# A two-layer graph network kernel: statistics a step ahead, transposes in the middle of aggregates, copies ahead of relus, adjacency chunks 4 to 6 issued behind DMA transposes

## The reference, cut to what matters

```python
def layer0(h, adj, s, weight, wgt_alpha, act_alpha, act_alpha2):
    w_norm   = (weight - mean(weight)) / std(weight, ddof=1)
    weight_q = weight_quant(w_norm, wgt_alpha, 3 bits)     # integers -7..7 times a step
    xq       = act_quant(h, act_alpha, 4 bits)             # integers up to 15 times a step
    support  = relu(xq @ weight_q)                         # 2048 x 512
    sup_q    = act_quant(support, act_alpha2, 4 bits)
    return adj @ sup_q                                     # 2048 x 2048 x 512

h = maximum(layernorm(x), 0);  x = x + layer0(h, adj, ...)
h = maximum(layernorm(x), 0);  x = x + layer1(h, adj, ...)
```

## Time and profile before

| | |
|---|---|
| runs, us | 157.33, 157.59, 158.1 |
| the profiled execution | 158.1 us, span 156.3 us, mean granted clock 0.986 |
| PE, PEld | 141.1 us (90%), 110.9 us (71%) |
| DVE, ACT, POOL | 108.5 us (69%), 108.3 us (69%), 30.1 us (19%) |
| moved by DMA | 27.44 MB, mean 176 GB/s |

### The profile page before, as it was taken

One profiled execution on the slowest core, in us unless ns is written; L12 is line 12 of the kernel. 1 busy time (PEld: TensorE's weight loads), 2 busy tenths in 40 slices (PEclk: granted clock), 3 DMA queues, 4 the chain that ended last, 5 costly groups with the idle time before them and its releaser, 6 DMA issues.

```text
span 156.3 us, 2088 instructions
## 1 busy us (share of the span) xinstructions
PE 141.1 (90%) x704; PEld 110.9 (71%) x704; DVE 108.5 (69%) x210; ACT 108.3 (69%) x137; POOL 30.1 (19%) x57
## 2 busy tenths in 40 slices
PE   0399999898999999999999999999999999999930
PEld 0395756565757667888888888888888888889920
DVE  0789978995966439997853686696779778624451
ACT  3587896896998779805955999999997977011000
POOL 2351232332020000016100101101105256011010
PEclk9999999999999999999999999999999999999995
DMA  5999999993315100080199899997101101110102
GB/s 146 331 420 423 396 388 419 430 306 38 67 38 67 34 0 0 0 273 0 17 268 415 258 361 376 377 351 268 69 0 67 71 0 67 67 67 0 67 8 71
DMA packets 11837, 27.44 MB, mean 176 GB/s; under 512 B 5040, under 2 KB 5296, under 8 KB 9776
## 3 DMA queue, kind: packets, MB, share of 16 engines
q1 hardware_dynamic: 11680, 27.01, 51.2%
q10 hardware_dynamic: 144, 0.26, 0.7%
HBM read 22.03 MB, written 4.19 MB: 168 GB/s over the span
## 4 chain that ended last, share of the span: by engine, by line
PE 72%; DVE 9%; DMA 7%; issue 6%; ACT 2%; POOL 1%; POOLq 0%; ACTq 0%; DVEq 0%
PE acc L930 26%; PE acc L932 26%; PE acc L912 7%; PE acc L913 6%; PE acc L898 5%; DMA h_iT<-h_i 4%; DMA w_sb<-weight 2%; DVE st L686 2%; DVE lo L721 1%; PE acc L940 1%; DVE w_st L749 1%; ACT hi L351 1%; ACT ring L371 1%; DVE h_i L710 1%; DVE mv L691 1%
## 5 line engine op out<-in xcount | busy, mean ns | idle before, releaser
L930 PE MATMUL acc<-sup,hi 128*128 128x512 f32 (+1 forms) x208 | 76.4, 374 | 0.1
L932 PE MATMUL acc<-sup,lo 128*128 128x512 f32 (+1 forms) x208 | 76.2, 373 | 0.0
L930 PEld LDWEIGHTS acc<-sup,hi 128*128 128x128 f32 x208 | 39.2, 188 | 7.3 <-issue 0.5
L932 PEld LDWEIGHTS acc<-sup,lo 128*128 128x128 f32 x208 | 39.2, 188 | 6.8
L363 ACT ACTIVATE junk<-raw,below 128x2048 uint8<-128x2048 f32 x16 | 31.8, 1985 | 0.0
L726 DVE TENSOR_TENSOR lo<-raw,hi 128x2048 fp32r<-128x2048 f32 x11 | 25.2, 2288 | 7.0 <-ACT hi L356 7.0
L912 PE MATMUL acc<-sup,hi 128*128 128x512 f32 x64 | 27.4, 428 | 0.7 <-DVE sup L715 0.7
L398 ACT ACTIVATE ring<-x_sb,nm 128x512 f32<-128x512 f32 x15 | 10.5, 716 | 23.1 <-POOL nm L509 19.6
L509 POOL TENSOR_SCALAR nm<-mv 128x1 f32<-128x1 f32 (+1 forms) x12 | 10.2, 847 | 83.4 <-DVE ve L696 83.4
L913 PE MATMUL acc<-sup,lo 128*128 128x512 f32 x64 | 25.1, 392 | 0.0
L356 ACT ACTIVATE hi<-raw 128x2048 fp32r<-128x2048 f32 x11 | 20.9, 1904 | 0.2 <-PE acc L913 0.2
(11 more groups left out here) (66 smaller groups left out, 83.1 us busy)
## 6 DMA issues: line engine op xcount, KB each, us to landing
raw<-adj_t SPq DMA_DIRECT2D x16, 1024.0 KB, 7.1
out<-ring SPq DMA_DIRECT2D x15, 256.0 KB, 4.9
x_sb<-x SPq DMA_DIRECT2D x3, 1024.0 KB, 14.0
w_sb<-weight SPq DMA_DIRECT2D x4, 258.0 KB, 4.3
x_sb<-x SPq DMA_DIRECT2D x1, 512.0 KB, 6.2
x_sb<-x ACTq DMA_DIRECT2D x1, 256.0 KB, 4.0
x_sb<-x SPq DMA_DIRECT2D x1, 256.0 KB, 5.3
out<-ring SPq DMA_DIRECT2D x2, 128.0 KB, 2.4
```

Of the source, the lines that this page charges most:

```text
L930: nc.tensor.matmul(bank[:, cols], part(hi, k % PARTS, j), sup[:, j, cols], start=(j == 0), stop=False)
L932: ins = nc.tensor.matmul(bank[:, cols], part(lo, k % PARTS, j), sup[:, j, cols], start=False, stop=(j == T - 1))
```

## The change

- VectorE: stats(7) and normalise(5) come ahead of the loop, right behind stats(6), and quantise_sup(2) ahead of quantise_h(4); in steps 4 and 5 the statistics are one tile further on, step 4 does quantise_sup(3) before two of them, step 5 one ahead of quantise_sup(4). From step 6 on the order is as before.
- ScalarE: split_piece(3) goes ahead of relu1(4); in steps 4 to 7 split_piece(j) goes between relu_sup(j-1) and copy_T(j), ahead of the relu1s of the step.
- PE: in steps 4 to 7 the transposes of tile j stand in the middle of aggregate_first(j-2), between rows 0, 1 and rows 2, 3. aggregate_first and aggregate do all hi matmuls of their rows (or of the tile) first and wait for the lo part only then.
- SP: only chunk 3 is issued ahead of the DMA transposes; chunks 4, 5 and 6 are issued behind transposes 8, 9 and 10.

```diff
             load_x(5)
-            for k in range(3, RAW):
-                load_adj(k)
+            load_adj(3)
             for j in range(TURN, T):
                 sp.wait_ge(hq_ready, j + 1)
                 if j >= TURN + 2:
                     sp.wait_ge(hqT_ready, j - 1)
                 sp.dma_start_transpose(h_iT[:, j % 2, :, :], h_i[:, j % SLOTS, :]).then_inc(h_turned[j % 2], 16)
+                if j - TURN + GT < RAW:
+                    load_adj(j - TURN + GT)
...
             copy_T(2)
             copy_T(3)
+            split_piece(3)
             relu1(4)
             relu_sup(2)
             relu1(5)
-            split_piece(3)
             for j in range(4, T + 2):
                 if j <= T:
                     relu_sup(j - 1)
+                if j < TURN:
+                    split_piece(j)
                 if j < T:
                     copy_T(j)
...
-                if j < T - 2:
+                if TURN <= j < T - 2:
                     split_piece(j)
-                elif j <= T:
+                elif T - 2 <= j <= T:
...
             lo_of_piece(2)
             stats(6)
+            normalise(5, stats(7))
+            quantise_sup(2)
             quantise_h(4)
-            quantise_sup(2)
-            nxt = 7
+            nxt = 8
...
-                for n in range(2 if j <= 5 else 1):
-                    if n == 1:
-                        quantise_sup(j - 1)
+                if j == 4:
+                    quantise_sup(j - 1)
+                for _ in range(2 if j == 4 else 1):
                     if nxt < T:
...
-                if 5 < j <= T:
+                if 4 < j <= T:
                     quantise_sup(j - 1)
...
                 pe.wait_ge(hi_piece, j + 1)
+                for t in rows:
+                    at = (j % GT) * GT + t
+                    nc.tensor.matmul(acc[t][:, :], part(hi, k % PARTS, at), sup[:, j, :], start=(j == 0), stop=False)
                 pe.wait_ge(lo_piece, j + 1)
                 for t in rows:
                     at = (j % GT) * GT + t
-                    nc.tensor.matmul(acc[t][:, :], part(hi, k % PARTS, at), sup[:, j, :], start=(j == 0), stop=False)
                     ins = nc.tensor.matmul(acc[t][:, :], part(lo, k % PARTS, at), sup[:, j, :], start=False, stop=(j == T - 1))
...
-                if j % GT == GT - 1 and j < T - 1:
+                if j % GT == GT - 1 and j < T - 1 and rows[-1] == GT - 1:
                     ins.then_inc(chunk_used, 1)
...
                 wait_hi(pe, k)
-                wait_lo(pe, k)
...
                         nc.tensor.matmul(bank[:, cols], part(hi, k % PARTS, j), sup[:, j, cols],
                                          start=(j == 0), stop=False)
+                    wait_lo(pe, k)
+                    for j in range(T):
                         ins = nc.tensor.matmul(bank[:, cols], part(lo, k % PARTS, j), sup[:, j, cols],
...
                 if j < TURN:
+                    aggregate_first(j - 2, range(GT // 2))
                     transposes(j)
-                aggregate_first(j - 2)
+                    aggregate_first(j - 2, range(GT // 2, GT))
+                else:
+                    aggregate_first(j - 2)
```

## The result

The changed kernel took 156.47 us, median of 8 runs (156.03 to 158.66), against 157.53 us of the kernel before (8 runs): ratio 0.992, interval 0.9897 to 0.9944. The forecast was 156.1 us, range 155.4 to 157.5. Two later sets of runs of the same file gave less: 156.79 against 157.58 and 156.94 against 157.77, so 0.8 us or 0.5% each.

A forecast was written before the change was run, and what follows sets the result against it. TensorE's matmul stream and its interruptions were taken as the bound. Terms of -1.40 to support(8) and -0.24 at aggregate(4) gave -1.64; with 0.1 kept back, 157.59 - 1.5 = 156.1 us, range 155.4 to 157.5.

The forecast's parts named there:

- What bounds the kernel: TensorE's matmul stream plus interruptions; nearly all loss between 15.8 and 38.05 us, plus one wait at 61.88.
- Start of aggregate(2), +0.41: TensorE up to support(4): aggregate(2) starts 0.11 later and transpose group 4 costs 0.30, so support(4) comes 0.41 us later.
- Statistics and copies, -0.50 and -0.62: Steps from support(4) to support(6): earlier statistics and copies ahead of relus remove waits, gaining 0.50 and 0.62 us.
- Transposes in the middle with thin cover; the wait on sup(5), +0.09: TensorE, support(6) to support(7): copies have 0.15 us cover, and aggregate(5) waits on sup(5); costs 0.09 us.
- Rival 1: Copies of transposed tiles stay on TensorE's path, supports waiting 0.2 us in each of four steps; 157.1 us, chance 0.12.
- copy(8) no longer waits, -0.78: ScalarE at support(8): transpose 8 lands at 31.9, before copy(8) at 35.5, so its DMA wait goes; gains 0.78 us.
- Sum up to support(8): Terms from the first aggregate on: support(8) starts at 36.65 instead of 38.05 us, -1.40.
- Hi before lo, -0.24 at aggregate(4), nothing for banks: TensorE's aggregates: aggregate(4) no longer waits for the last lo piece, -0.24 us; changed bank order costs 0.
- Chunks behind transposes: SP's queue: with chunks 4 to 6 behind transposes 8 to 10, transposes 9 to 11 land in time, 0.4 us spare.
- rival 3: SP's queue: only transpose 11 late, by up to 1.9 us; 156.3 to 158.0, 157.2 in the middle; chance 0.11.
- the prediction's own signs: Among signs of being wrong: copy(9), (10) or (11) waiting on h_iT, pointing to late DMA transposes; no size given.
- -1.64 for the stretch: First aggregate to aggregate(4): -1.40 up to support(8) plus -0.24 at aggregate(4), before 0.1 was kept back.

The follow-up runs named there:

- again: The changed kernel run and profiled once more with no edit; median 156.79 us, 0.9945 of the kernel before.
- chunk6_last: The changed kernel with chunk 6 issued behind transpose 15 instead of transpose 10; 156.11 us, 0.991 of the kernel before.
- u_stats: chunk6_last with VectorE's order of the kernel before (statistics not ahead); 156.96 us, 0.9956 of the kernel before.
- u_act: chunk6_last with ScalarE's order of the kernel before (pieces behind the relus); 156.26 us, 0.9888 of the kernel before.
- u_mid: chunk6_last with transposes ahead of the aggregates and quantise_h(4) ahead of quantise_sup(2); 155.88 us, 0.9885 of the kernel before.
- u_hilo: chunk6_last with hi and lo matmuls in pairs and the lo wait ahead of both; 156.21 us, 0.989 of the kernel before.
- chunks_only: The kernel before with only SP's new issue order; 157.29 us, 0.9992 of the kernel before.
- best: The same file as u_mid, run again beside the changed kernel on one chip; 155.47 us, 0.9864 of the kernel before.
- after_third: The changed kernel run a third time, no edit, on one chip with best; 156.94 us, 0.9947 of the kernel before.

## Why the prediction was right, and the step that was mis-sized

1. *What bounds the kernel*: right. The change's effect lies between the first aggregate and aggregate(4); from there to the end 94.3 to 94.4 us in each.
2. *Start of aggregate(2), +0.41*: measured +0.48 (support(4) 9.03 after the first aggregate in *again*, 8.55 before), +0.58 and +0.57 in the two other profiles of the changed kernel, +0.41 in chunk6_last.
3. *Statistics and copies, -0.50 and -0.62*: -0.47 and -0.63. u_stats shows that the statistics carry it; by u_act ScalarE's order gives 0.13 in one step.
4. *Transposes in the middle with thin cover; the wait on sup(5), +0.09*: +0.02, and no support waited for h_qT in those steps. Rival 1 (157.1) didn't happen. That this part costs and doesn't gain was in the sum (+0.3 of the +0.41), and the three profiles of u_mid's order put it at 0.10 to 0.40.
5. *copy(8) no longer waits, -0.78*: -0.78. Sum up to support(8): -1.40 forecast, -1.38 measured.
6. *Hi before lo, -0.24 at aggregate(4), nothing for banks*: 0.24 there by u_hilo, and nothing for banks.
7. *Chunks behind transposes, "nothing is late, with 0.4 us to spare at the last"*: this failed, and it is rival 3, "only transpose 11 is late", that happened in part: 0.79 us in *again*, 0.18 to 0.90 over three profiles. By the prediction's own signs (a wait of copy(11) on h_iT) this part was wrong. The mechanism was the one worked out (transpose 11 behind chunk 6); the term mis-sized was the chunk's time to landing. I took 4.8 us for each from one row, chunk 7 of the kernel before, issued at 65.89 with an empty queue. Chunks 4 to 6 took 5.4, 6.2 and 6.8 in *again*. Chunk 6, issued at 37.4 in the replay, then lands at 44.2 instead of 42.2. A second term was off the other way: transpose 11 landed 0.5 to 0.6 us after chunk 6 in all three profiles, not the 1.0 to 1.5 of the replay. So it lands at 44.8, 0.7 past the 44.1 when it was needed; without this second error it would have been 1.1 to 1.6 late.

Why the chunks took longer is shown only in part. Chunk 7 of *again*, issued at 64.76 with nothing in flight, took not 4.8 but

```profile
raw<-adj_t SPq DMA_DIRECT2D x1, 1024.0 KB, 5.8
```

and the same chunk took 4.8 in chunks_only, 5.7 and 5.9 in the two other profiles of the changed kernel and 6.3 in best. So the 4.8 was the short end of what a lone chunk takes, and about 1 us of the 2.0 was in that choice; the rest came with chunk 5, transpose 10 and transpose 11 in the queue beside it, which no run separates. Rival 3 also has a slip in its sum: 37.4 + 6.4 + 2.4 is 46.2, so 2.1 late and not 1.9.

So -1.64 for the stretch became -0.65, -0.86 and -1.42 in three executions of the changed kernel, and the median moved by 1.06 us where 1.5 was forecast, by 0.8 in each of the two later sets. That the time stayed near the forecast has some luck in it: the transpose's shorter delay behind the chunk paid for part of the chunk's longer time, and nothing in the forecast bounded how far the wait would differ between executions. chunk6_last, without that wait, has -1.72.

The Trainium skill's rule (DMA: Bandwidth & Descriptors, Queues, rings and completion order) is that a semaphore write lands only after every earlier write of its DMA engine. The rows agree: transpose 11 landed 0.57 us after chunk 6 in *again*, where that took 6.8 us, and 0.58 in after_third, where it took 6.2.

## What to carry to other kernels

When a bulk load is moved off one small transfer that was late behind it, find the next small transfer that it will stand ahead of, and price the load by the longest row on record and with the queue as full as it will then be, not by a single row (the lone 1 MB chunk took 4.8 to 6.3 us here, chunks 4 to 6 of the changed kernel 5.4 to 6.9); then place the load by its own due time (chunk 6 was needed only near 60 us, over 20 us after its issue) rather than behind the first gap. A group of small instructions is best put in front of a wait that exists anyway: in the middle of a run of matmuls it costs its full price (about 0.3 us for four transposes). Gains too small for the medians can be read at one instruction of the profile: support(8) came 0.78 us earlier with SP's part alone, 0.55 with the others alone and 1.38 with all, while the medians (0.1%, 0.5%, and 0.5 to 0.8%) can't say whether the parts add up.

## What the runs showed of the hardware that I had not expected

The start varies by up to 1.95 us between executions of kernels with the same start on PE: in the profiles the first aggregate started from 15.23 to 17.18 us. Behind the first transposes stand 34 warm-up matmuls of 128 columns; they took from 2.19 to 3.83 us. PE's timeline of chunk6_last and then of the first profile of the changed kernel:

```profile
9.74 2.19 PE L950 MATMUL acc<-ident 128*128 128x128 bf16 x34
```

```profile
10.12 3.83 PE L949 MATMUL acc<-ident 128*128 128x128 bf16 x34
```

In the first, most of these matmuls start 0.056 us apart; in the second, all of them 0.107. That is a factor of two, the factor between the two levels of PE's clock, 2.4 and 1.2 GHz: 128 columns in 0.107 us are 1.2 columns a ns. The windows of PE (busy us, matmuls that touch the window, granted clock, DMA share, GB/s) seem to speak against it, for they print 1.00 in both, here chunk6_last:

```profile
10.00:11.00 1.00, 1.00 (x21) 1.00 0.93 371
```

and the changed kernel:

```profile
10.00:11.00 1.00, 1.00 (x13) 1.00 0.87 352
...
12.00:13.00 1.00, 1.00 (x13) 1.00 1.06 408
```

| profile | last spacing of 0.107 starts | first clock record | 34 warm-ups took | first aggregate |
|---|---|---|---|---|
| chunk6_last | 9.85 | 9.99 | 2.19 | 15.49 |
| after_again | 11.57 | 11.68 | 3.09 | 15.29 |
| before | 11.98 | 12.08 | 3.03 | 15.81 |
| best | 13.05 | 13.21 | 3.62 | 16.12 |
| after_third | 14.01 | 14.16 | 3.81 | 16.85 |
| changed, first profile | 14.49 | 15.24 | 3.83 | 17.18 |

(In the last row the matmuls from 14.60 on are the first supports, of 512 columns: they start 0.43 us apart up to 15.03 and 0.22 apart from 15.35 on, so the clock rose between.) Where the clock rose by 12.1 us, the first aggregate started between 15.23 and 15.81; the four later rises (best, u_act and the last two rows) gave 16.12 to 17.18. The transposes of tile 1 stand behind the 34 warm-ups and start at 12.07 in chunk6_last, at 13.74 in the first profile, so the late rise of the clock explains the late start. What sets the time of the rise no run here shows. The late start passes into the time: between the first profile and *again* the start differs by 1.89 us and the span by 2.1, between best and u_mid by 0.85 and 1.2.

The first DMA transpose of the changed kernel, with an empty queue ahead of it, took 3.2 us (3.5 in the first profile), not the 2.4 of an isolated one in the earlier trace rows. Being first is not enough to explain it, for in chunks_only and best it took 2.5; and most profiles have one more lone transpose among the later ones that took longer (3.6 in the kernel before, 4.4 in chunk6_last). None of these made PE wait, but a transpose that is due 2.4 us after its issue can't be counted on.
